# Pair 15 of the second attention in block 2's banks, the value-bias product on GpSimd, blank products moved, and a new order of steps

## The reference, cut to what matters

```python
z  = _mha(x, x, Wq1, Wk1, Wv1, mask0, causal=True)          # block 1
x1 = _layernorm(x + z, ln1_g, ln1_b)
z  = _mha(x1, context, Wq2, Wk2, Wv2, mask1, causal=False)   # block 2
x2 = _layernorm(x1 + z, ln2_g, ln2_b)
z  = jnp.maximum(x2 @ fc1_w.T + fc1_b, 0.0) * mask0
z  = (z @ fc2_w.T + fc2_b) * mask0
x  = _layernorm(x2 + z, ln3_g, ln3_b)
qh, kh, vh = (heads of q @ wq + bq, k @ wk + bk, v @ wv + bv)   # second attention
scores  = einsum(qh / 8, kh) + bias + graph_attn_bias
weights = softmax(scores)
out = (weights @ vh) @ wo + bo + residual
out = layernorm(out) * ln_g + ln_b
```

## Time and profile before

| | |
|---|---|
| median of 3 runs | 341.96 us (341.45 to 343.37) |
| the profiled execution, its own time | 341.61 us |
| its span in the trace | 339.8 us |
| TensorE busy | 320.3 us (94%) |
| VectorE busy | 291.3 us (86%) |
| ScalarE busy | 239.9 us (71%) |
| GpSimd busy | 241.6 us (71%) |
| mean granted TensorE clock | 0.995 of full |

### The profile page before, as it was taken

One profiled execution on the slowest core, in us unless ns is written; L12 is line 12 of the kernel. 1 busy time (PEld: TensorE's weight loads), 2 busy tenths in 40 slices (PEclk: granted clock), 3 DMA queues, 4 the chain that ended last, 5 costly groups with the idle time before them and its releaser, 6 DMA issues.

```text
span 339.8 us, 13231 instructions
## 1 busy us (share of the span) xinstructions
PE 320.3 (94%) x5328; PEld 252.3 (74%) x5333; DVE 291.3 (86%) x836; ACT 239.9 (71%) x567; POOL 241.6 (71%) x376
## 2 busy tenths in 40 slices
...
GB/s 154 332 327 210 3 0 2 3 65 4 2 4 133 2 4 2 88 57 12 54 4 3 2 141 4 11 3 33 103 2 5 0 143 3 3 17 136 2 2 31
DMA packets 13180, 17.87 MB, mean 53 GB/s; under 512 B 1601, under 2 KB 10177, under 8 KB 13121
## 3 DMA queue, kind: packets, MB, share of 16 engines
...
## 4 chain that ended last, share of the span: by engine, by line
PE 56%; DVE 26%; ACT 5%; issue 5%; POOL 4%; DMA 1%; SPq 1%; POOLq 0%; ACTq 0%; DVEq 0%
PE C_E L632 5%; PE C_E L577 4%; PE B_E L451 3%; PE C_E L622 3%; PE A_E L432 3%; PE B_E L432 3%; PE C_E L593 2%; DVE A_mx L889 2%; PE A_E L451 2%; DVE A_S L897 2%; PE C_E L609 2%; PE B_E L465 2%; DVE Sc L973 2%; DVE C_den L991 2%; DVE L_xh L943 2%
## 5 line engine op out<-in xcount | busy, mean ns | idle before, releaser
L1025 POOL TENSOR_TENSOR A_kblk<-A_qk,cst 128x1024 f32<-128x1024 f32 x16 | 30.3, 1897 | 25.5 <-DVE A_qk L865 25.4
L1046 POOL TENSOR_TENSOR L_xg<-L_xh,vec_sb 128x128 f32<-128x128 f32 x64 | 29.2, 456 | 15.9 <-DVE L_xh L943 13.9
L1035 POOL TENSOR_TENSOR L_rstd<-L_ve,cst 128x1 f32<-128x1 f32 x64 | 35.1, 548 | 5.0
L1077 POOL TENSOR_TENSOR Sc<-Sc,C_mx 128x512 f32<-128x512 f32 x28 | 29.1, 1046 | 9.4 <-DVE C_mx L983 9.3
L763 ACT ACTIVATE qT<-C_E,bq 128x128 f32<-128x128 f32 x112 | 31.9, 379 | 4.1 <-PE C_E L577 3.9
L1033 POOL TENSOR_TENSOR L_ve<-L_mv,cst 128x1 f32<-128x1 f32 x64 | 12.1, 189 | 29.4 <-DVE L_mv L930 28.8
L1086 POOL TENSOR_TENSOR Pc<-Pc,C_rd 128x512 f32<-128x512 f32 x28 | 29.0, 1043 | 2.8 <-DVE C_rd L993 2.5
L1025 POOL TENSOR_TENSOR B_kblk<-B_qk,cst 128x1024 f32<-128x1024 f32 x16 | 30.3, 1897 | 0.0
L577 PE MATMUL C_E<-x3T,wq_sb 128*128 128x128 f32 x224 | 29.6, 279 | 0.4 <-ACT x3T L755 0.4
L577 PEld LDWEIGHTS C_E<-x3T,wq_sb 128*128 128x128 f32 x224 | 27.0, 192 | 1.1 <-ACT x3T L755 0.7
L632 PE MATMUL C_E<-wo_sb,C_zT 128*128 128x128 f32 x224 | 27.5, 276 | 0.1
...
## 6 DMA issues: line engine op xcount, KB each, us to landing
...
```

Source lines behind the costliest of these rows:

```text
L1025: tt(a.kblk[:], a.qk[:, 1].unsqueeze(1).to_broadcast([P, 8, P]), at["rmask"].unsqueeze(2).to_broadcast([P, 8, P]), ALU.mult).then_inc(a.s_ ...
L1035: tt(l.rstd[:], l.ve[:], at["power"], ALU.pow).then_inc(l.s_rstd, 1)
L1046: tt(l.xg[:], l.xh[:], l.g, ALU.mult).then_inc(l.s_xg, 1)
L1077: tt(v, v, place(n).mx[:, 8 * g:8 * g + 8].unsqueeze(2).to_broadcast([P, 8, S]), ALU.subtract).then_inc(C.s_sub, 1)
```

## The change

It has four parts. All that is not shown is the list `PLAN`, which is written anew as a whole.

1. Pair 15 of C gets a third place, `own[2]`: the banks and tiles of B (`Bc.EE`, `Bc.S`, `Bc.PT`, `Bc.kblk`) and `wv_sb` for its output. `C.x3t#15` now waits for the second norm of pair 15 to have read B's bank, and `C.q_0#15` no longer for `C.y#13`.
2. The value-bias product: a new step `C.bvw` on GpSimd multiplies all of `wo` by `bv` and adds the eight slices down to two, in three dependent instructions that use the tile `Pc` before the second attention needs it. `C.bvo` then has two products in place of eight.
3. There are eight `L.warm` steps in place of six. They write to `Bc.J`, and wait for the third norm of pair 15 in place of the second.
4. A new order of all steps.

```diff
-COOL = 6
+COOL = 8
...
+        "ones": np.ones((P, 1)),
...
-        own = [Chain(), Chain()]
+        own = [Chain(), Chain(), Chain()]
         for k, o in enumerate(own):
-            o.EE = (C.EE, A.EE)[k]
+            o.EE = (C.EE, A.EE, Bc.EE)[k]
...
-            o.S = A.S if k else sb("Sc", [P, H * S])
-            o.P = A.S if k else sb("Pc", [P, H * S])
-            o.PT = A.PT if k else sb("PTc", [P, H * S])
-            o.qT = A.kblk if k else sb("qT", [P, J, P])
-            o.zT = (wk_sb if k else sb("C_zT", [P, HD]))[:].rearrange("p (j b c) -> p j b c", b=2, c=S)
+            o.S = (A.S, Bc.S)[k - 1] if k else sb("Sc", [P, H * S])
+            o.P = (A.S, Bc.S)[k - 1] if k else sb("Pc", [P, H * S])
+            o.PT = (A.PT, Bc.PT)[k - 1] if k else sb("PTc", [P, H * S])
+            o.qT = (A.kblk, Bc.kblk)[k - 1] if k else sb("qT", [P, J, P])
+            o.zT = ((wk_sb, wv_sb)[k - 1] if k else sb("C_zT", [P, HD]))[:].rearrange("p (j b c) -> p j b c", b=2, c=S)
...
         def place(n):
+            if n == PAIRS - 1:
+                return own[2]
             return own[n % 2 if n >= SPLIT else 0]
...
-            return n - 2 if n > SPLIT + 1 else -1
+            return n - 2 if SPLIT + 1 < n < PAIRS - 1 else -1
...
-                pe.wait_ge(L2.s_xh, PAIRS)
-                idle_products(Bc.X[:, :], 3)
+                pe.wait_ge(L3.s_xh, PAIRS)
+                idle_products(Bc.J[:, :], 3)
...
-                pe.wait_ge(w_out, 16 * 2)
+                pe.wait_ge(bvw_ready, 3)
                 pe.wait_ge(C.s_vs, 2 * FIRST)
-                for j in range(J):
-                    last = mm(own[0].E[0][:, 0:D], bv_sb[:, j:j + 1].to_broadcast([P, P]), wo_sb[:, j],
-                              start=(j == 0), stop=(j == J - 1))
+                for j in range(2):
+                    last = mm(own[0].E[0][:, 0:D], at["ones"].to_broadcast([P, P]), own[0].P[:, j * D:(j + 1) * D],
+                              start=(j == 0), stop=(j == 1))
...
+                elif n < PAIRS - 1:
+                    pe.wait_ge(C.s_zts, 2 * n - 2)
                 else:
-                    pe.wait_ge(C.s_zts, 2 * n - 2)
+                    pe.wait_ge(L2.s_xh, PAIRS)
...
-                    elif g == 0 and n > 1 and n != SPLIT + 1:
+                    elif g == 0 and n > 1 and n not in (SPLIT + 1, PAIRS - 1):
...
+            def bvw(n):
+                pool.wait_ge(w_out, 16 * 2)
+                w = own[0].P
+                tt(w[:].rearrange("p (j d) -> p j d", d=D), wo_sb[:], bv_sb[:].unsqueeze(2).to_broadcast([P, J, D]),
+                   ALU.mult).then_inc(bvw_ready, 1)
+                pool.wait_ge(bvw_ready, 1)
+                tt(w[:, 0:4 * D], w[:, 0:4 * D], w[:, 4 * D:8 * D], ALU.add).then_inc(bvw_ready, 1)
+                pool.wait_ge(bvw_ready, 2)
+                tt(w[:, 0:2 * D], w[:, 0:2 * D], w[:, 2 * D:4 * D], ALU.add).then_inc(bvw_ready, 1)
...
-K.warm#0 A.qkv#0 K.warm#1 A.qk#0 A.q0#0 A.e0#0 A.nz#0 A.cnt#0 C.whi#0 K.warm#2 A.cut#0 A.v#0 C.chi#0 K.warm#3
```

More of the change, by code:

```diff
@@ L1104 @@
 PLAN = """
-K.warm#0 A.qkv#0 K.warm#1 A.qk#0 A.q0#0 A.e0#0 A.nz#0 A.cnt#0 C.whi#0 K.warm#2 A.cut#0 A.v#0 C.chi#0 K.warm#3
-A.kblk#0 K.warm#4 C.wlo#0 A.qkv#1 C.clo#0 C.wvhi#0 A.e#0 C.k_0#0 A.qk#1 A.max_0#0 A.max_1#0 C.k_1#0 C.ks_0#0
-A.q0#1 A.sub_0#0 A.e0#1 C.ks_1#0 A.sub_1#0 C.k_0#1 A.exp_0#0 A.nz#1 A.exp_1#0 A.cnt#1 A.pt_0#0 A.cut#1
-A.pt_1#0 A.pts_0#0 A.v#1 C.k_1#1 A.kblk#1 A.pts_1#0 A.m0#0 C.ks_0#1 A.pv_0#0 A.pv_1#0 C.wvlo#0 A.qkv#2 A.zts#0
-C.ks_1#1 A.z#0 C.k_0#2 C.chi#4 A.zn#0 C.k_1#2 A.y#0 C.ks_0#2 A.st#0 C.ks_1#2 C.k_0#3 A.rstd#0 C.k_1#3 C.ks_0#3
@@ L1260 @@
-C.rstd#15 C.xh#15 C.gb#15 C.store#15
+A.qkv#0 A.qk#0 A.q0#0 A.e0#0 A.nz#0 A.cnt#0 K.warm#0 A.cut#0 C.whi#0 A.v#0 K.warm#1 A.kblk#0 C.chi#0 C.wlo#0
+A.qkv#1 K.warm#2 C.clo#0 A.e#0 A.m0#0 K.warm#3 A.qk#1 A.max_0#0 C.k_0#0 C.wvhi#0 A.q0#1 A.max_1#0 K.warm#4
+C.k_1#0 C.ks_0#0 A.sub_0#0 A.sub_1#0 A.exp_0#0 A.e0#1 A.exp_1#0 A.pt_0#0 A.nz#1 C.ks_1#0 A.cnt#1 A.pt_1#0
+A.v#1 C.k_0#1 A.pts_0#0 A.cut#1 A.pts_1#0 C.wvlo#0 A.pv_0#0 C.ks_0#1 A.kblk#1 A.pv_1#0 C.k_1#1 A.zts#0 A.z#0
+C.k_0#2 C.ks_1#1 A.zn#0 C.k_1#2 A.y#0 C.ks_0#2 A.st#0 A.qkv#2 C.ks_1#2 A.rstd#0 C.k_0#3 C.k_1#3 A.xh#0
@@ new lines @@
+A.y#3 A.st#3 C.v_1#3 B.qk#2 B.y#1 C.vs_0#3 A.rstd#3 B.q0#2 B.st#1 B.e0#2 C.vs_1#3 A.v#4 B.rstd#1 C.x3t#0
+B.nz#2 C.bvo#0 A.xh#3 C.x3ts#0 B.cnt#2 B.xh#1 A.e#4 B.v#2 B.gb#1 C.obias#0 B.cut#2 A.qkv#5 A.gb#3 A.max_0#4
+B.f1#1 C.q_0#0 A.qk#5 A.max_1#4 B.kblk#2 B.f1s#1 A.sub_0#4 B.f2#1 C.q_1#0 B.f2s#1 B.am#3 A.exp_0#4 A.sub_1#4
+B.f3#1 C.qs_0#0 B.e#2 B.y3#1 A.q0#5 B.3st#1 A.exp_1#4 A.e0#5 B.max_0#2 C.qs_1#0 B.3rstd#1 A.pt_0#4 B.max_1#2
+A.pt_1#4 B.cm#3 B.sub_0#2 C.e#0 A.pts_0#4 B.3xh#1 A.pts_1#4 B.sub_1#2 B.3gb#1 B.exp_0#2 A.pv_0#4 A.nz#5
```

304 lines of the change are left out of this document (150 added, 154 removed).

## The result

The changed kernel takes **343.67 us** (median of 19 runs, all but one between 342.94 and 344.72; the one, 442.1, is left out of the ratio), the kernel before 341.76 beside it. The ratio is 1.0052, interval 1.0043 to 1.0062: slower by 0.5%, 1.8 us (the medians lie 1.9 apart). The forecast was 339.8 and the range 337.4 to 342.9, so both are wrong. The profiled execution has 343.46 us of its own and a span of 341.7 us, 1.9 above the span before.

The account below looks back on a forecast made before the run. The prediction took full engines (TensorE, VectorE) to bound the middle and pair 15's dependent chain the end. Its terms, -1.0 - 0.6 - 0.7 + 0.5 = -1.8 us against 341.6, gave 339.8 us, range 337.4 to 342.9.

Parts of the forecast that it names:

- The value-bias product: Two TensorE products for eight before A.e#4: -1.0 us, ends 0.7 and 1.5, GpSimd's three added instructions costed at nothing.
- The order in the middle: Between 51 and 289 us: the 0.85 us wait of B.tr#6 goes, -0.6 us; nothing for the rest, bounds -4.7 and +2.
- my rival: In the middle: two new waits the size of that at 121.83 us, giving 341.2 us; chance 0.17.
- The end: Pair 15 of C starts 0.6 us sooner and blank products ahead of B.f2#15 go: -0.7 us, ends 0.2 and 1.3.
- The blank products: At the start, the pair between C.k_0#0 and C.k_1#0 lies where TensorE had no gap: +0.5 us.
- `A.m0#0`: At the start, now ahead of A.max_0#0, so the maxima begin about 1 us late: taken as zero, upper end +0.9.
- both clock rivals: At the start, TensorE's clock rises during A.e#0 (341.6 us, chance 0.17) or stays low until C.k_1#0 (344.0, chance 0.08).
- what would show it: Signs to check, among them value-bias product at a quarter of 2.02 us and blanks behind A.cnt#0 at 378 ns, not 600.
- The order gives back what the parts gain: In the middle: two new waits, as one gone on one full engine appears on the other; 341.2 us, chance 0.17.
- The rival at 344.0: At the start, TensorE's clock stays low until C.k_1#0, still at the lower level at 15 us: +4.2 us, chance 0.08.

Follow-up runs that it names:

- e2_bvo: d1_both without C.bvw on GpSimd, the value-bias product again as eight products on TensorE in the same place; 342.21 us, ratio 1.0005.
- s1_parts: The kernel before, old order, with only the value-bias product changed (three GpSimd instructions, two products on TensorE); 343.61 us, ratio 1.0059.
- d1_both: The changed kernel with A.kblk#4 moved behind B.3gb#0 on GpSimd and C.xh#8 moved behind C.max_0#10 on VectorE; 341.50 us, ratio 0.9993.
- f1_four: The changed kernel with A.m0's second instruction as four of one column, the start's blank products in old places, C.xh#8 behind C.max_0#10; 339.96 us.
- f3_oldfour: The kernel before with one edit, A.m0's second instruction written as four of one column; 340.56 us, ratio 0.9963.
- e3_tail: d1_both up to B.f1#14, behind it the old order with two places and the old blank products; 342.56 us, ratio 1.0014.
- e1_warm: d1_both with the five blank-product steps of the start back in their places of the kernel before; 341.34 us, ratio 0.9983.
- s3: The changed kernel with the new order up to B.f1#11, then the old order, two places and old blank products at the end; 343.01 us, ratio 1.0037.
- s4: The changed kernel with A.kblk#4 on GpSimd moved behind B.3gb#0; 343.57 us, ratio 1.0055.
- f4: The changed kernel with the norm C.xh written as a tensor_scalar with two per-partition scalars; 343.38 us, ratio 1.0030.
- d3: The changed kernel with the column of ones written by VectorE's memset instead of loaded with the constants; 346.40 us, ratio 1.0138.
- e4: The changed kernel, order untouched, with A.m0's second instruction (128x4) written as four of one column; 342.03 us, ratio 1.0006.

## Why the prediction was wrong, by its own steps

**The value-bias product (-1.0).** The sign was right, the size was too large: 0.4 to 0.7, where the prediction's low end was 0.7. TensorE and GpSimd of the changed kernel, against the earlier trace rows:

```profile
61.49 0.68 PE L370 MATMUL C_E<-Pc,cst 128*128 128x128 f32 x4
```

```profile
50.39 1.90 POOL L1073 TENSOR_TENSOR Pc<-wo_sb,bv_sb 128x1024 f32<-128x1024 f32 x1
52.37 1.27 POOL L1076 TENSOR_TENSOR Pc<-Pc 128x512 f32<-128x512 f32 x1
53.71 0.73 POOL L1078 TENSOR_TENSOR Pc<-Pc 128x256 f32<-128x256 f32 x1
55.07 0.19 POOL L1038 TENSOR_TENSOR L_ve<-L_mv,cst 128x1 f32<-128x1 f32 x1 [0.62 <-DVE L_mv L935]
```

The two products took 0.68 us, a third of the 2.02 and not the quarter. The part is worth 0.9 on the spot and 0.4 at the end (e2_bvo). The cover held, since 0.62 us of idle time stand behind it, though the two additions took 1.27 and 0.73 us and not the 0.95 and 0.47 of a proportional estimate. By s1_parts, without it the part costs more than it gives.

**The order in the middle (-0.6, "and nothing for the rest").** This step failed. The wait of 0.85 us for `B.tr#6` is gone, as forecast. The rest was not nothing: the middle, from the first `C.x3t` to the last `B.3gb`, grew from 254.2 to 256.2 us. I had bounded the new waits by +2, and my rival had two of 0.85. Two holds that cost 1.3 each came, and one of 0.5 at 168 us. (The first of the three lies ahead of the first `C.x3t`, at 61.35 us, and d1_both, without the two large ones, still has 255.6 us there; so the shifts, not this distance, say what the holds cost.) With the holds out, the gap's -0.6 did not arrive either: by the spans f1_four is 0.4 below f3_oldfour, and the value-bias part (0.4) and the end (0.7), less the start that is 0.4 late, would give 0.7, so that the new order of the middle lost some 0.3, as far as such a sum over several kernels can tell.

The cause lies in the step above it. The prediction named the rule that GpSimd contends with VectorE, as it stood there only for instructions with two SBUF inputs, which `A.m0`'s is not, and then asked only what VectorE does beside the *added* 3.3 us. There it was right: nothing on VectorE grew between 50.4 and 54.4 us. The same question was not put to the steps that the order *moved*: `A.kblk#4`, of which it said only when `h` would be ready, and `A.kblk#15`. And it took the earlier trace rows for a slowing in proportion. GpSimd's row at that time says otherwise:

```profile
9.43 1.89 POOL L1025 TENSOR_TENSOR A_kblk<-A_qk,cst 128x1024 f32<-128x1024 f32 x1 [8.99 <-DVE A_qk L865]
```

`C.wlo` began at 10.24, and from GpSimd's end at 11.32 to its own at 12.41 are 1.09 us, about the 1.21 of its twin: it waited and then ran at its usual pace. `A.m0` had the same in the trace of before. Its second instruction took 0.17 to 1.03 us in its four places, and each long one ended with an instruction of GpSimd, as here:

```profile
115.78 1.03 DVE L838 TENSOR_SCALAR m0s<-am 128x4 f32<-128x4 f32 x1
```

```profile
114.89 1.90 POOL L1025 TENSOR_TENSOR B_kblk<-B_qk,cst 128x1024 f32<-128x1024 f32 x1
```

**The end (-0.7).** Right, in mechanism and size. GpSimd and TensorE of the changed kernel:

```profile
317.55 0.46 POOL L1058 TENSOR_TENSOR h<-L_xg,vec_sb 128x128 f32<-128x128 f32 x1
```

```profile
318.06 0.33 PE L569 MATMUL B_E<-cst,h 128*128 128x128 f32 x1 [0.25 <-POOL h L1058]
...
322.75 1.16 PE L598 MATMUL B_E<-kT,B_kblk 64*64 64x64 f32 x64
```

`C.x3t#15` begins 0.05 us behind `h`, where it was 0.65, and the distance from it to the end is 23.6 for 23.4 us. e3_tail gives 0.7 for the whole.

**The blank products (+0.5) and `A.m0#0` (0).** The first was too high: e1_warm and d1_both differ by 0.1 in the profiles, 0.16 in the medians and 0.3 by the ratios. The maxima of pair 0 began at 13.83, 1.0 late, as worked out, though 0.3 of it is a hold of `A.m0#0` (0.49 in place of 0.17 us); the three kernels with the blanks in their old places are still 0.2 to 0.5 late at `B.f1#0`, so zero was a little low, inside its bound.

**The rivals.** The clock was low at the start of the changed kernel's profile, but not in the way of the rival. Windows of the changed kernel, the clock as third last number:

```profile
7.00:8.00 1.00, 0.45 (x9) 0.45 (x11) 0.49 (x4) 0.00 (x0) 0.00 (x0) 0.81 1.00 358
8.00:9.00 1.00, 0.61 (x12) 0.45 (x11) 0.29 (x1) 0.00 (x0) 0.00 (x0) 0.50 1.24 300
```

Its products at 5 us ran at the short duration; after an idle stretch of 1.89 us TensorE was granted 0.50, its lower level (1.2 GHz), and had 1.00 again from 11.0 us, ahead of `A.e#0` at 11.78. The four blanks there took 622 ns each, so by the list of "what would show it" this was wrong too. What it cost here doesn't show: the shift at pair 0 is 0.4, and it is 0.4 in f1_four too, which has no such drop. In other profiles with the new start the conditions of both clock rivals were met: where the clock rose during `A.e#0` (s3, s4, e3, f4), `B.f1#0` was 0.7 to 1.3 us late against the 1.8 of the rival, and where it rose behind 15 us (d3, e4) 2.5 and 2.9 late against 4.2. "The order gives back what the parts gain" had the right sign and the wrong agent. The rival at 344.0 comes nearest to the measured 343.67, but that is luck: its condition, TensorE at the lower level at 15 us, was not met in this profile. No rival had an existing instruction that grows.

**The account.** Holds in the changed kernel: 1.3 + 0.5 (`A.m0`, e4_m0four) + 1.3 (`C.xh#8`, d1_both) = 3.1. In the kernel before: 1.2 (f3_oldfour). With `A.m0` free on both sides, `C.xh#8` moved and the blank products of the start in their old places, the change is worth 339.96 - 340.56 = -0.6. The sum is 3.1 - 1.2 - 0.6 = +1.3. The new places of the blank products add 0.1 to 0.3 (e1_warm), against 1.8 to 1.9 measured. The rest, 0.2 to 0.5 us, no run accounts for; holds that were measured in different kernels need not add up. That f1_four lands on the forecast's 339.8 is chance: 1.2 of its 1.75 us come from a line that the change did not touch.
